# New step lists for four interleaved chains of a two-layer decoder, and a list for the load and store queue

## The reference

```
x += L0_attn(LN(x))    windowed attention, 7 positions, 16 heads of 16; projections q, k, v, out
x += L0_xattn(LN(x))   16 heads against ctx_1024 (128 tokens), mask on both sides, one projection
x += L0_ffn(LN(x))     64 slots: route with top 8, gather, a GRU step on the slots, spread back
x += L1_attn(LN(x))    causal attention with a position bias, 16 heads, projections
x += L1_xattn(LN(x))   16 heads against ctx_1024, projections
x += L1_ffn(LN(x))     int8-like quantized 256 -> 1024, depthwise conv of 3 taps, SiLU, quantized 1024 -> 256
```

## Time and profile before

| | us |
|---|---|
| median of 3 runs (lowest to highest) | 3631.13 (3620.27 to 3642.56) |
| the profiled execution | 3635.76 |
| its span, first to last instruction | 3633.8 |
| PE busy | 3113.3 (86%) |
| DVE busy | 2590.4 (71%) |
| ACT busy | 2178.2 (60%) |
| POOL busy | 555.5 (15%) |
| granted TensorE clock, mean of full speed | 0.943 |

### The profile page before, as it was taken

One profiled execution on the slowest core, in us unless ns is written; L12 is line 12 of the kernel. 1 busy time (PEld: TensorE's weight loads), 2 busy tenths in 40 slices (PEclk: granted clock), 3 DMA queues, 4 the chain that ended last, 5 costly groups with the idle time before them and its releaser, 6 DMA issues.

```text
span 3633.8 us, 64290 instructions
## 1 busy us (share of the span) xinstructions
PE 3113.3 (86%) x25516; PEld 2222.2 (61%) x25516; DVE 2590.4 (71%) x5788; ACT 2178.2 (60%) x4268; POOL 555.5 (15%) x1040
## 2 busy tenths in 40 slices
PE   2589987899889998899888998899988998879995
PEld 1446764577556666567665666566655676656663
DVE  4575678765896568875888667866788657886667
ACT  1236863477645775566755676557764577646773
POOL 0231002210121101211022101211012110122000
PEclk9789998999989999999999999889999999989996
DMA  3000000000000000000000000000000000000000
GB/s 130 30 1 1 1 14 21 8 1 4 11 21 9 1 4 21 11 8 1 14 19 11 1 4 11 21 8 1 11 14 11 8 1 14 11 11 8 1 4 9
DMA packets 45965, 45.28 MB, mean 12 GB/s; under 512 B 11120, under 2 KB 43632, under 8 KB 45536
## 3 DMA queue, kind: packets, MB, share of 16 engines
q1 hardware_dynamic: 45664, 41.17, 3.8%
HBM read 32.77 MB, written 8.39 MB: 11 GB/s over the span
## 4 chain that ended last, share of the span: by engine, by line
PE 61%; DVE 19%; ACT 11%; issue 4%; DMA 3%; POOL 2%; SPq 1%; DVEq 0%; POOLq 0%; ACTq 0%
PE banks L1172 9%; PE banks L1203 9%; PE banks L1249 6%; PE banks L1311 5%; PE banks L1212 4%; PE banks L1245 3%; PE banks L1332 3%; DVE chain_m L670 2%; PE banks L1275 2%; PE banks L1188 2%; PE banks L1290 2%; DVE chain_arena L747 2%; DVE chain_arena L875 2%; ACT chain_arena L1006 2%; PE banks L1390 2%
## 5 line engine op out<-in xcount | busy, mean ns | idle before, releaser
L670 DVE TENSOR_REDUCE chain_m<-banks 128x4 f32<-128x512 f32 x512 | 332.6, 684 | 192.4 <-PE banks L1203 191.3
L1203 PE MATMUL banks<-chain_arena 64*128 64x256 f32 x3072 | 448.2, 415 | 24.5 <-DVE chain_m L670 12.2
L1203 PEld LDWEIGHTS banks<-chain_arena 64*128 64x128 f32 x3072 | 280.6, 194 | 155.3 <-issue 93.8
L1027 ACT ACTIVATE chain_arena<-chain_arena,chain_m 128x128 f32<-128x128 f32 x1024 | 323.8, 395 | 77.9 <-DVE chain_m L670 77.2
L1500 POOL TENSOR_TENSOR chain_rs<-chain_rv,neg_half 128x2 f32<-128x2 f32 x192 | 147.5, 768 | 1360.6 <-DVE chain_ng L655 1359.7
L1249 PEld LDWEIGHTS banks<-chain_arena 64*128 64x128 f32 x4096 | 256.8, 193 | 113.3 <-issue 113.3
L1249 PE MATMUL banks<-chain_arena 64*128 64x128 f32 x4096 | 306.9, 291 | 0.0
L961 ACT ACTIVATE chain_xn<-chain_xa,chain_nm,chain_rs 128x256 f32<-128x256 f32 x384 | 209.5, 596 | 152.4 <-POOL chain_nm L1503 151.4
L668 DVE TENSOR_TENSOR chain_arena<-banks,pos_bias 128x512 f32<-128x512 f32 x256 | 175.2, 684 | 149.7 <-PE banks L1203 149.3
L1212 PE MATMUL banks<-chain_arena,chain_va 128*32 128x128 f32 x5120 | 194.2, 278 | 34.1 <-ACT chain_arena L1006 21.3
L1006 ACT ACTIVATE chain_arena<-banks,chain_mask_k 128x1024 f32<-128x1024 f32 x128 | 142.9, 1117 | 109.5 <-PE banks L1249 109.0
(11 more groups left out here) (310 smaller groups left out, 6968.3 us busy)
## 6 DMA issues: line engine op xcount, KB each, us to landing
chain_xn<-in_ctx SPq DMA_DIRECT2D x32, 256.0 KB, 3.0
chain_xa<-in_x SPq DMA_DIRECT2D x32, 256.0 KB, 3.2
out<-chain_xa SPq DMA_DIRECT2D x32, 256.0 KB, 2.2
chain_arena<-in_mask SPq DMA_DIRECT2D x32, 128.0 KB, 3.7
rel<-in_rel SPq DMA_DIRECT2D x1, 2048.0 KB, 8.4
f_w1t<-in_w1t SPq DMA_DIRECT2D x1, 1024.0 KB, 7.7
f_w2t<-in_w2t SPq DMA_DIRECT2D x1, 1024.0 KB, 10.1
wqkv0T<-in_wqkv0T SPq DMA_DIRECT2D x1, 768.0 KB, 4.5
```

The costliest lines, as they stand in the source:

```text
L670: e.tensor_reduce(t["m"][:, b, r, :], t["s"][:, u % 4] if bias else bank(c, u % 2), AX.X, ALU.max, negate=True).then_inc(*done(f"{tag}_mx{ ...
L1027: ex = e.activation(s, s, ACT.Exp, bias=t["m"][:, u // GROUPS, row_group(u), a:a + 1])
L1203: mm[i] = e.matmul(c.ps[:, i, 2 * T * j:2 * T * j + 2 * T], t["qh"][p, j, x, b, :], flat(t["kx"][p, j, b]), start=not masked, stop=not mas ...
```

## The change

All four lists of `ORDER` are other ones; their lengths, and how often each digit stands in them, are the same (in the PE list 776 times each). A fifth list, `sync`, is new. It has 64 digits: `sync_turn` is cut by two `yield`s into two steps, the load of the context and the rest, and `sync_program` follows the list through `in_order`. No instruction of any engine is added, removed or altered, no buffer and no wait either.

```
 ORDER = {
+    "sync": (
+        "0011223313210320131320201132302011323020113230201132302011323020"),
     "pool": (
-        "0120312301230101200121330122233013201323010210023113220003311001220021101122132320321330332132301302"
...
+        "1321032013201132302013120320132013201320131231120330221110033113121232313230200132020002132032101301"
...
@@ -1571,6 +1573,7 @@
     if n:
         e.wait_ge(*c.dve.of(prior)("g_q2"))
     e.dma_start(t["xn"][:], dram["ctx"](n)).then_inc(c.ctx, 16)
+    yield
     if n:
         e.wait_ge(*c.dve.of(prior)("y1"))
         e.dma_start(dram["out"](prior), t["xa"][:]).then_inc(c.store, 16)
@@ -1642,9 +1646,7 @@
             setup_sync(e, k, inp, ld)
             set_up(e)
             e.wait_ge(cleared, 3 * NCHAIN)
-            for n in range(TURNS):
-                for i, ch in enumerate(chains):
-                    sync_turn(e, ch, n, dram(i))
+            in_order(ORDER["sync"], lambda c, n: sync_turn(e, chains[c], n, dram(c)))
```

More of the change, by code:

```diff
@@ new lines @@
+        "1321032013201132302013120320132013201320131231120330221110033113121232313230200132020002132032101301"
+        "1323321101223031131100331223321300220122300200302102103113233110210122133110031332233213002201223002"
+        "0030210210311323311021012213311003133223321300220122300200302102103113233110210122133110031332233213"
+        "0022012230020030210210311323311021012213311003133223321300220122300200302102103113233110210122133110"
+        "031332233213002201223002003021021031132330202200"),
```

175 lines of the change are left out of this document (87 added, 88 removed).

## The result

The changed kernel takes **3513.35 us** (3508.93 to 3515.35, 4 runs) against 3632.29 for the kernel before in the same session (3620.27 to 3642.56, 4 runs): ratio 0.9672, 95% interval 0.964 to 0.9704. The forecast was 3569, in a range of 3480 to 3650. So the sign was right and the size was half: 62 us of span were forecast, 126.8 came (3633.8 to 3507.0).

A forecast was written before the change was run, and what follows sets the result against it. PE was taken to set the pace, busy 86%, its idle time spread in short pieces. 531.8 + 2905.9 + 132.7 + 1.5 = 3571.9 us of span gave a 3569 us median, range 3480 to 3650.

The forecast's parts named there:

- to the end of chain 1's first turn: Set-up and first turn: set-up untouched, then 361 PE steps at the old 1.117 us, ending at 531.8 us.
- its seven turns behind that, to 3395.4: The seven turns after the first: 2679 PE steps at 1.0847 us, 2905.9 us, against 2983.6 at the old pace.
- drain and last stores: Program end: drain of 132.7 us, 13.6 less than before, plus 1.5 us for four stores standing behind chain 0.
- take the best stretch: 0.989 + 0.096: Seven turns: PE busy 0.989 and idle 0.096 us a step, as in the third stretch, 420.9 us a turn.
- the clock's share, 27 us: PE's clock over the program: a fuller PE might raise it, another 27 us, kept for the range's low end.
- The condition that I gave for failure: PE in the turns: the prediction fails if busy time a step leaves 0.98 to 1.00 us.
- the case that I gave 0.50: Repeated turns: the forecast itself, turns of 413 to 428 us, chance 0.50.
- much faster: Rival for the seven turns: PE nearly full at 1.045 us a step, 3463 us in all, chance 0.18.
- Whoever may pick one turn and repeat it can do as well as the best of six: Reason for the seven turns' price: one repeated turn can match the best of six differing stretches, idling 0.096 a step.
- SP's list at 0: SP's new order of context loads: costed at 0, with 57 us the most that could go or come back.
- nothing won: Rival for the seven turns: still 1.1137 us a step, 3649.6 us of span or 3647 median, chance 0.20.
- slower: Rival: uncovered product and next scores on PE, repeated, cost 8.3 us a turn, 3704 in all, chance 0.12.

The follow-up runs named there:

- e3: The changed kernel with only SP's list altered, so each chain's two SP steps stand together as in the old order under the new chain order: 3516.69 us, 0.9674.
- e1: All five lists made from the fourth turn of the kernel before, repeated every 422 us of planned time: 3886.94 us, ratio 1.07.
- e12: e1 with the four chains set apart by 64, 57 and 43 us as in the changed kernel, not 73, 59 and 108: 4365.43 us, 1.2029.
- e10: All four lists made from the fifth turn of the kernel before, repeated every 430 us of planned time: 3858.24 us, 1.0625.
- e8: The changed kernel plus three tiny unneeded ACT activations in one place per turn, forcing four table loads in a row (5.1 us): 3721.61 us, 1.0252.
- e9: The changed kernel plus unneeded ACT activations in two places per turn, two table loads each (2.6 us): 3650.09 us, 1.0056.
- e2: The changed kernel's fifth turn, taken by trace times, in all eight turns, start and end too: 3506.6 us, 0.9652.
- e6: The changed kernel's fifth turn, taken by places in the lists instead of times, repeated through the program: 3505.32 us, 0.9643.
- e5: The changed kernel with 12 pairs of PE-list digits swapped, putting another chain's step between a chain's product and its next scores: 3535.45 us, 0.9729.
- e4: The kernel before with SP's steps split by the two yields and a list loading each context ahead of other chains' stores: 3631.1 us, 0.999.

## Why the prediction came out as it did

Set against the terms of the sum, on the span (forecast 3571.9, measured 3507.0):

| term | forecast | measured | difference |
|---|---|---|---|
| to the end of chain 1's first turn | 531.8 | 539.75 | +8.0 |
| its seven turns behind that, to 3395.4 | 2905.9 | 2855.7 | -50.2 |
| drain and last stores | 134.2 | 111.6 | -22.6 |

**The seven turns: the step that failed is "take the best stretch: 0.989 + 0.096".** The second turn took 406.7 us for 362 steps, 14.0 over the forecast; the third 398.7 for 377, 10.2 under; the last five, of 388 each, 410.05 on the mean and not 420.9, together 54.0 under. Of these 1.057 us a step some 0.963 are busy once the missing records are put back (370.5 + 3.1 us in 388 steps) and 0.094 idle; e3 has 0.963 and 0.099. So the idle time was right to 0.003 us a step, and that was in part luck: the stretch that it was read from, repeated as it stands, idles 67.8 us a turn (e1), 0.175 a step. The busy time was not right: I had held 0.989 fixed as a property of the work, and put the clock's share, 27 us, into the low end only, "since the clock of the best stretch is hardly over the others". It is a property of the order. The condition that I gave for failure, busy time outside 0.98 to 1.00, is what happened. A turn of 410 us also lies under the 413 to 428 of the case that I gave 0.50; 1.057 a step is nearer to the 1.045 of "much faster" than to the 1.085 of the forecast.

Traces with all their records show this across the orders, per repeated turn of 388 steps (the kernel before: the mean of the six stretches of the earlier trace rows and the one behind them, 378.37 busy us of 426.6):

| | turn | busy | idle | clock |
|---|---|---|---|---|
| e12 | 522.2 | 407.7 | 114.5 | 0.89 |
| e1 | 460.8 | 393.0 | 67.8 | 0.93 |
| e10 | 457.4 | 387.6 | 69.8 | 0.94 |
| before | 432.1 | 383.7 | 48.4 | 0.94 to 0.96 |
| e8 | 436.9 | 381.1 | 55.8 | 0.95 to 0.96 |
| e9 | 425.9 | 376.5 | 49.3 | 0.97 to 0.98 |
| e3 | 411.8 | 373.5 | 38.3 | 0.98 to 0.99 |

Busy time follows the clock without exception. Busy time times clock is 363 to 367 us in every row, an estimate from the table by which the clock carries nearly all of the difference. The clock follows the sum of the idle time only roughly: e9 idles as long as the kernel before and has the better clock and 7.2 us less busy time, and e10 idles 2 us longer than e1 and has the better clock too. What about the old order's pauses makes them cost more clock than e9's, their length or their place between other work, no run here tells apart. The single matmul shows the same: L1245 has a mean of 393 ns before and 384 in e3 (as L1247), L1254, the same line in e8, 410. The shortest and the median are 377 and 379 ns in all three and the longest 631 to 634, so more of these matmuls run slow; it is not that each of them is a little slower.

The Trainium skill (TensorE: Matmul & The Clock Gate, Part 1) has the slow clock as the default that activity lifts, so that a gap costs a second time; e8 agrees, with 8.2 us beside 17.7. By that rule I had named a sum 27 us lower, 3542; that was a third of the 79.1 us. My price for it (0.010 busy us a step for 0.02 of clock) came from two stretches of the same order, where it hid behind different work: the fourth and the sixth stretch, at the same 0.96 as the third, have 0.974 and 0.985 busy us a step, and the third 0.991. Over the table e1 against e3 gives (393.0 - 373.5) / 388 = 0.050 for 0.055 of clock, nearly twice as much.

**"Whoever may pick one turn and repeat it can do as well as the best of six"** was the reason for the number, and it is not the reason for the gain. e2 and e6 show that a single turn is enough for all of it. e1 and e10 show that a turn that was not fitted to follow itself loses 25 to 29 us a turn. What is left is the fit of each step to the other three chains and the other engines. For it speak e5 (swap 12 pairs of 3104 digits, and 22 us are gone) and e12 (keep each chain's order and move the chains against each other, and 478 more are gone than in e1). What in the new order makes the fit, and so the better clock, no run takes apart.

**The first turn** was priced at the old 1.117 a step and took (539.75 - 128.9) / 361 = 1.138. PE is busy in it for 359.7 us, or 1.005 a step with the missing records put back, as before (1.006); what rose is the idle time, from 0.111 to 0.133 a step. The window from 500 to 700 us lies mostly in the second turn, the one that took 14.0 over the forecast. The repeated turn from the start (e6) needs 370 us for 324 steps, 1.142, which is no better, but at step 1100 it stands at 1320.9 us and the changed kernel at 1345.2; in its longer turns and the end it gives back all but 8 of these 24.

**The drain.** 79 steps at 1.38 us were to take 108.8 and took 89.4: I used the pace of 75 steps with 793 matmuls beside them, and there were 543. Windows of the two kernels' stretches, first before, then after:

```profile
3487.50:3590.80 103.30, 84.57 (x793) 60.92 (x792) 69.02 (x139) 61.24 (x112) 7.40 (x20) 0.89 0.02 6
```

```profile
3395.40:3484.80 89.40, 60.77 (x543) 43.74 (x547) 71.17 (x150) 50.92 (x84) 6.52 (x16) 0.87 0.00 1
```

The pace of DVE steps was the wrong unit where PE still had its own work to do. The 11 steps alone took 17.3 us and not 21.3. That was a slip of reading: they begin with the last but one L920, at 3613.50, not at 3609.93, and from there the kernel before needs 17.7. The four stores cost 4.8 us behind the last `y1` where 4.1 were in the sum.

**What was right:** equal distances from turn 4 on, within 2 us, in the trace of the changed kernel; some 37 idle us in such a turn; SP's list at 0 (e3, e4); 66 table loads; four stores within 2 us; fewer waits of DVE for the masks. That the distances are so equal is partly chance: e3, with the same four lists, has turns of 409.3 to 413.5 us, and e6 of 409.8 to 413.5. My sign of failure, turns of one list that differ by several us, is thus there with no harm to the forecast. **The rivals:** "nothing won" and "slower" did not come. The second's mechanism is there at its place, at 0.9 us a wait of PE. It had been priced by the waits of DVE and ACT at 1.82 and 1.31 us, and these fell, to 1.53 (127.0 / 83) and 1.14 (148.7 / 131), and became fewer, though more steps have no cover; waits of DVE for other lines of PE grew in their place (for L1313 127.3 us after 83.9, for L1292 106.9 after 53.5). And e5 shows that the price of a place can't be read as the gain of covering it. "Much faster" needed PE nearly full at 1.045; the turns came close, 1.057, by another way: more clock, not fewer gaps. The weight loads went from 2222.2 us to 2177.5 in e3, at 61% and 62%, and followed the clock as the matmuls did; they pointed to no room beyond the idle time. The Trainium skill (Perfetto Trace Analysis, Identifying the Most-Contended Engine) holds them for a better measure of the distance to the limit than the busy share of the matmuls; no run here can test that.

## What to carry to other kernels

Where one engine sets the pace and its gaps are short, the busy time in its row is not a constant of the work: price a new order by idle time and by the granted clock together, and take the clock's price from kernels of different pace, not from stretches of one. In a fully ordered program of interleaved chains a wait's length is not what covering it brings (12 and 15 such swaps lost time here); try a swap, don't sum waits. One well-fitted turn, repeated from first to last, did as well as lists made for the whole program.

## What the runs showed of the hardware

- The same 3178 matmul records of a repeated turn (3187 in e10) were busy for 371 to 408 us, with granted clocks from 0.99 to 0.89.
- Extra work on ACT alone (164 us in 128 table loads of 1283 ns in e8: the 96 of the first row below, and 32 of the second, which are 14 in the changed kernel) made PE's matmuls longer by 71 us in the whole program, 3034.2 to 3105.2.

```profile
L1014 ACT ACT_TABLE_LOAD x96 | 123.2, 1283 | 0.9
L1015 ACT ACT_TABLE_LOAD x46 | 59.0, 1283 | 11.4 <-PE banks L1258 11.1
```

- A list that is exactly periodic has turns that differ by up to 4 us (e6: 409.8 to 413.5), but where the turn is slower and more regular it repeats to 0.2 us from the second turn on (e1).
- Four stores of 256 KB issued together at the end landed in 2.6 us each at the median, against 2.1 when apart.
